# Two gate projections moved over the block boundary, and four Horner steps moved behind the masking products, in a Mamba-2 mixer

## The reference

```
x = x + mixer(layernorm(x))
x = x + mlp(layernorm(x))

mixer:  proj = h @ W_in * mup;  z, xBC, dt = split(proj)          # 1024, 1280 and 64 columns
        xBC = silu(causal depthwise convolution of 4 taps)         # x, B, C
        dt = softplus(dt + dt_bias);  dA = exp(-dt * exp(A_log))
        state = state * dA + (dt * x) outer B;  y = state . C      # 64 heads of 16, state of 128
        g = (y + D * x) * silu(z)
        out = (g * rsqrt(mean(g^2) + eps) * norm_w) @ W_out
mlp:    out = ((silu(h @ gate' * gs) * (h @ up' * us)) @ down') * ds   # inner width 1408
```

## Time and profile before

| | us |
|---|---|
| median of 3 runs | 861.14 (858.68 to 861.72) |
| the profiled execution | 859.09 |
| its span | 857.4 |
| PE busy | 763.8, 89% of the span |
| DVE busy | 525.5, 61% |
| ACT busy | 506.9, 59% |
| POOL busy | 301.3, 35% |

### The profile page before, as it was taken

How to read it: one execution, slowest core, us unless ns; L and a number is a source line. 1 busy time by engine, 2 the same in 40 slices (tenths; PEclk the granted TensorE clock), 3 DMA queues, 4 the chain that set the end, 5 groups by cost and what they waited for, 6 DMA issues and landing times. The chain is left out here.

```text
span 857.4 us, 20336 instructions
## 1 busy us (share of the span) xinstructions
PE 763.8 (89%) x8488; PEld 622.6 (73%) x8488; DVE 525.5 (61%) x840; ACT 506.9 (59%) x963; POOL 301.3 (35%) x247
## 2 busy tenths in 40 slices
PE   5786989989989999998998998554989999999997
PEld 5765778778768777777777776343867887887886
DVE  6865874975965984985985984572832442442341
ACT  6968786887877886887887886412631331331330
POOL 3055284274374364455455454223001101101002
PEclk9968999999999999999999999786989999999999
DMA  9614242452443253243253153752001201201102
GB/s 309 177 40 114 46 115 75 85 124 77 77 107 101 67 117 101 56 125 103 54 125 106 29 124 107 291 213 63 25 2 62 86 1 61 86 0 62 37 1 74
DMA packets 39196, 77.68 MB, mean 91 GB/s; under 512 B 9408, under 2 KB 15040, under 8 KB 39104
## 3 DMA queue, kind: packets, MB, share of 16 engines
q1 hardware_dynamic: 38784, 75.84, 32.0%
q10 hardware_dynamic: 320, 0.52, 0.3%
HBM read 67.43 MB, written 8.92 MB: 89 GB/s over the span
## 5 line engine op out<-in xcount | busy, mean ns | idle before, releaser
L409 POOL TENSOR_TENSOR ring<-tokd,ring 128x1024 f32<-128x1024 f32 x64 | 121.1, 1904 | 229.1 <-ACT tokd L571 190.1
L1051 PE MATMUL ps_proj<-xn_hi,win_hi 128*128 128x256 f32 x608 | 181.6, 299 | 17.5 <-ACT sz L520 13.9
L1052 PE MATMUL ps_proj<-xn_lo,win_hi 128*128 128x256 f32 x608 | 173.9, 286 | 0.0
L1053 PE MATMUL ps_proj<-xn_hi,win_lo 128*128 128x256 f32 x608 | 173.3, 285 | 0.0
L1051 PEld LDWEIGHTS ps_proj<-xn_hi,win_hi 128*128 128x128 f32 x608 | 117.7, 194 | 33.6 <-issue 15.8
L1052 PEld LDWEIGHTS ps_proj<-xn_lo,win_hi 128*128 128x128 f32 x608 | 117.9, 194 | 0.0
L1053 PEld LDWEIGHTS ps_proj<-xn_hi,win_lo 128*128 128x128 f32 x608 | 117.8, 194 | 0.0
L792 DVE SCALAR_TENSOR_TENSOR cx<-cin,consts,cx 128x256 f32<-128x256 f32 x240 | 97.5, 477 | 0.5 <-ACT cx L552 0.4
L1352 POOL TENSOR_TENSOR res<-res,hidden 128x512 f32<-128x512 f32 x16 | 20.5, 1282 | 189.1 <-DVE hidden L1427 189.1
L847 DVE TENSOR_TENSOR ring<-ring,ps_tok 128x1024 f32<-128x1024 f32 x64 | 75.6, 1213 | 17.6 <-ACT ring L580 17.6
L1384 ACT ACTIVATE silu_g<-pb,scales 128x512 f32<-128x512 f32 x44 | 30.3, 688 | 94.4 <-PE pb L1496 94.3
(11 more groups left out here) (150 smaller groups left out, 1530.1 us busy)
## 6 DMA issues: line engine op xcount, KB each, us to landing
ring<-cum_dram SPq DMA_DIRECT2D x128, 256.0 KB, 4.6
xin<-x SPq DMA_DIRECT2D x8, 512.0 KB, 4.1
res<-x SPq DMA_DIRECT2D x32, 128.0 KB, 2.6
x_in_sb<-x_dram SPq DMA_DIRECT2D x4, 1024.0 KB, 6.3
res<-x_dram SPq DMA_DIRECT2D x16, 256.0 KB, 2.6
out<-res SPq DMA_DIRECT2D x16, 256.0 KB, 2.0
x_dram<-res SPq DMA_DIRECT2D x28, 128.0 KB, 2.4
wg<-gate_w SPq DMA_DIRECT2D x4, 704.0 KB, 9.8
```

The costliest lines, as they stand in the source:

```text
L409: pool.tensor_tensor(ring[:, g, :, :], own, ring[:, g, :, :], ALU.subtract).then_inc(diffed, 1)
L1051: pe.matmul(out, win_hi[:, k, cols], xn_hi[:, k, :], start=(k == 0), stop=False)
L1052: pe.matmul(out, win_hi[:, k, cols], xn_lo[:, k, :], start=False, stop=False)
L1053: made = pe.matmul(out, win_lo[:, k, cols], xn_hi[:, k, :], start=False, stop=(k == KT - 1))
```

## The change

Three things move, and nothing is added or removed.

PE: `project(i, 6)` and `project(i, 7)` stood behind `turn_tok(i, 0)` and behind `turn_x(i, 0)` in their own block. They now stand at the end of the block before, behind its last `project_out`. `project(i, 8)` stood behind `group(c, 0)` and now stands before `carry(i, 0)`.

ACT: `evacuate(i, 6)` and `evacuate(i, 7)` stood behind the last `fade` of step 2i. `evacuate(i, 6)` is now the first instruction of the block, `evacuate(i, 7)` follows `square`, and `keep_tok` stands behind that. The first two clamps are ahead of `square`.

DVE: the Horner steps 4 to 7 stood between `mask_cb` and `make_xpad` of the second step. They now stand behind the four `mix` products, together with steps 8 to 11.

```
@@ scalar body @@
                 c = STEPS * i
-                keep_tok(c)
+                if not first:
+                    evacuate(i, 6)
                 clamp(c, 0)
+                clamp(c, 1)
                 if not first:
                     square(c - 1)
-                clamp(c, 1)
+                    evacuate(i, 7)
+                keep_tok(c)
                 fade(c, 0)
...
                 fade(c, 3)
-                if not first:
-                    evacuate(i, 6)
-                    evacuate(i, 7)
-                else:
+                if first:
                     for n in range(EARLY, PIECES):
@@ vector body @@
                 mask_cb(c)
-                for n in range(4, 8):
-                    soft(i + 1, n)
                 make_xpad(i, 1)
...
                 for g in range(1, GROUPS):
                     mix(c, g)
-                for n in range(8, LOGN):
+                for n in range(4, LOGN):
                     soft(i + 1, n)
@@ tensor body @@
                 turn_tok(i, 0)
-                if not first:
-                    project(i, 6)
                 turn_x(i, 0)
-                if not first:
-                    project(i, 7)
+                if first:
+                    pe.wait_ge(lo_made, EVENTS)
+                project(i, 8)
                 carry(i, 0)
...
                 group(c, 0)
-                if first:
-                    pe.wait_ge(lo_made, EVENTS)
-                project(i, 8)
                 group(c, 1)
...
                 project_out(c - 1, SECOND_HALF)
+                if not last:
+                    project(i + 1, 6)
+                    project(i + 1, 7)
```

## The result

The changed kernel takes 828.59 us (median of four runs, 826.47 to 829.62), the kernel before 861.43 (four runs, 858.68 to 861.8): a ratio of 0.962, 95% interval 0.959 to 0.965. The forecast was 836, and its range ended at 829. The gain is 32.8 us where I had 25.4; between the two profiled executions it is 859.09 - 829.62 = 29.5 us. Direction and mechanism came as forecast, the size did not. Of all executions behind the ratios of this document, two (1186 us of a later kernel, 1445 us of the kernel before) were in a slow state and are not counted in them.

A forecast was written before the change was run, and what follows sets the result against it. TensorE was taken as the bound, with two recurring holes. 13.9 + 8.9 + 3.0 - 2.8 - 1 + 3.4 = 25.4 us off 859.1 gave 833.7; with 2.05 added for the median, 836 us (831 to 840).

The forecast's parts named there:

- The wait for `sz`: TensorE before project(i,8), waiting for ScalarE's evacuation of a gate pair: all seven waits go, 13.9 us.
- that for `xpad` in blocks 1 to 6: TensorE before carry(i,1): the 1.46 us wait goes once Horner steps 4 to 7 move, 8.9 us in six blocks.
- block 0's: Block 0's `xpad` wait before its second carry: 4.20 us falls to some 1.2, a gain of 3.0 us.
- ACT's new order: ScalarE: keep_tok 5.19 us after gate_hi; rival: keep_tok 1 to 2 us later, 843 to 850 us, chance 0.09.
- At 68.07 in block 0: Block 0: keep_tok behind clamps and project(0,8) before a slow carry delay pair 8; 1 us lost, bounds 0 and 2.5.
- three signs of "wrong": Wrong if carry(i,0) waits over 1 us, eight Horner steps take over 3.5 us, or new stalls exceed 5 us.
- the step headed "Sum": Whole kernel: 13.9 + 8.9 + 3.0 - 2.8 - 1 + 3.4 = 25.4 us saved.
- "Nothing is added": TensorE: no work added; 48 matmuls (6.0 us) move to the block before and project(i,8) moves ahead of the carry.
- The new wait: TensorE before carry(i,0), for `xpad` behind the later keep_tok: 0.4 us seven times, 2.8 us lost.
- The clock: Slow TensorE stretches behind waits in blocks 1 and 4 and at a carry: 3.4 us gained, bounds 0 and 4.3.
- More stalls: Rival, TensorE's steady part: two more "issue" stalls, 3.1 us each plus 1.4 us slow clock, 845 us; chance 0.12.
- The steps beside POOL: Rival, VectorE: fade_state slows the eight Horner steps to 0.76 us each, 861 us (chance 0.04), or 892 (0.02).

The follow-up runs named there:

- the gate part alone: The changed kernel with Horner steps 4 to 7 put back ahead of `xpad`, so without the DVE move: 841.47 us, ratio 0.979 against the kernel before.

## Why the prediction was right in kind and 7.4 us short

**Right, with its numbers.** The wait for `sz` went (13.9 us), that for `xpad` in blocks 1 to 6 too (8.9), and block 0's fell from 4.20 to 1.30 us (2.9, forecast 3.0). ACT's new order had the slots that I gave it (5.15 us to keep_tok, forecast 5.19), no table load came between, and the steps missed fade_state by 0.6 us. At 68.07 in block 0 0.85 us were lost, for which 1 was taken. Each of the three signs of "wrong" stayed away: no wait over 1 us at carry(i,0), eight steps in 2.57 us, and no more stalls than before.

**Where it failed: the step headed "Sum".** The starts of turn_tok(1,0) and turn_tok(7,0), before and after:

```profile
109.59 0.27 PE L1081 MATMUL ps_tok<-eye,cx 128*128 128x128 f32 x1
...
502.82 0.27 PE L1081 MATMUL ps_tok<-eye,cx 128*128 128x128 f32 x1
```

```profile
112.04 0.27 PE L1079 MATMUL ps_tok<-eye,cx 128*128 128x128 f32 x1
...
481.58 0.27 PE L1079 MATMUL ps_tok<-eye,cx 128*128 128x128 f32 x1
```

turn_tok(1,0) starts 2.45 us later (109.59, then 112.04), but two projections, some 5.8 us, have moved ahead of it, so 3.3 us were gained there (forecast 3.1). From there to turn_tok(7,0) it gained 393.23 - 369.54 = 23.7 (forecast 20.4), and behind that 8.3 less the same 5.8 = 2.5 (forecast 1.9). So 4.1 us are missing from the sum, 3.3 of them in the steady part:

- *"Nothing is added" on TensorE was taken as "the work keeps its length".* It does not. Block 4 is 5.30 us shorter, and its waits and its slow projection give 2.26 + 1.46 + 1.45 - 0.24 = 4.93; the other 0.37 us are starts that lie closer. Projections 6 and 7 take 2.84 us each in the changed kernel, from one start to the next (353.69, 356.53, 359.36), where in the kernel before they took 2.95 behind turn_tok and 3.00 behind turn_x. What stands ahead makes the difference: behind an output product (as 6 now does) or another projection (as 7 does) the second matmul starts 0.12 us after the first, behind turn_tok, turn_x or a group 0.20 to 0.23. Groups 0 and 1 in a row take 308.84 to 310.25 = 1.41 us, apart 0.79 + 0.80. In six blocks 2.2 us are left over, of which 0.7 are the stall, shorter by chance or by a cause that no run shows (2.42 us for 3.13); the closer starts are the other 1.5 us: the largest term that was missing.
- *The new wait* was 0.72, 0.23, 0, 0.24, 0.24, 0.47 and 0.24 us, in all 2.1 for a forecast of 2.8; 0.5 of it in the six blocks.
- *The clock.* I took 3.4 of the 4.3 us, "as block 0 keeps a wait". It keeps 1.30 us, and the carry behind it ran in 1.94 us, at full clock: the upper bound was right, and 0.5 us more of it fell to the steady blocks than I had in the sum.

The new neighbours of projections 6 and 7 were in the order of instructions, and the spread of projection lengths, 2.95 to 3.09 us by what stands ahead and behind, was in the trace; I did not ask where it came from.

**The other 3.1 us are not in the mechanism.** I added 2.05 us, since the profiled execution of before lay that far under the median. The changed kernel's profiled execution lay 1.03 above its own median. The second profiles took 859.99 and 829.29 us, and the kernel before ran between 854.3 and 863.7 us in its undisturbed runs. That is scatter of single executions, and nothing allowed it to be carried over as a constant with its sign: without it the forecast is 833.7, against 829.62 of the profiled execution. Taken from the medians alone, my 25.4 would have given 861.43 - 25.4 = 836, and with the 4.1 us 832; the last 3.3 us to 828.59 are in no trace, and by the spread of the runs they can be scatter.

**What the sum hid.** I added the terms as if each could be had alone. The runs show that they can't: the Horner part alone is worth 0 us, the gate part alone 18, and all but project(i,8)'s move 0. That the sum came as near as it did has luck in it. The forecast came near only because all of it was done at once and every chain that could have taken the place of a hole (keep_tok, the last gate, the end of the second half) moved with it.

**The rivals.** More stalls: not seen; the stall sits at the same instruction in all but one of the kernels whose waits are shown here, the `turn_tokd` in the second half of block 2 with 5 of 16 products to go (turn_tokd(3,0) in the program; the expectations above call it turn_tokd(4,0)). ACT's new order: not seen. The steps beside POOL: the mechanism is real, 23 us when it is brought about, and 0.6 us of distance kept it away here. Its price per step was wrong (one long wait, not eight slow steps), and it left out what the clock adds.

What stays open: why a wait of about 2.2 us was followed by a slow clock in two or three cases of six in one kernel, a wait of 2.1 us in seven of seven in another, and one of 2.72 us in a third not at all; and what the stall is. One thing in the traces bears on it: in all ten profiles that have the stall, a 16 KB packet of the DMA queue that the profile calls "instruction" starts 2.6 to 2.8 us before the products go on, and takes 1.3 us; in the one without it, the packet starts 4.9 us before the transposition. That the products wait for it is a guess that no run tests.

## What to carry to other kernels

Where several waits recur in one loop, find which chain would be late next before adding them up: the first fix may be worth nothing alone and the second most of it. When a step moves, its new neighbours on the same engine count too, since an instruction can start sooner behind one than behind another. Look at what the products behind each TensorE wait take, and price the wait with them, and leave the distance between one profiled execution and the median out of the sum unless it repeats.

## What was not expected of the hardware

- A vector instruction that meets a POOL instruction can be held for all that is left of it: 3.76 us, in two blocks, and 2.88 us in five for a Horner step of 0.29 us beside fade_state. GPSIMD Engine Reference of the Trainium skill, Specifications, has the contention that this agrees with; that it takes one instruction whole, and leaves the others as they are, is what the run shows.
- The cost of a hole is not its length, nor is it settled by it. In the steady blocks the granted clock was low behind two or three of six waits of 2.2 us, behind all six of 2.65 us, all six of 3.1 us and more, and, ahead of a carry, all seven of 2.1 us; behind waits of up to 1.5 us, the one of 1.90 and the one of 2.72 us ahead of a carry it was not. In the kernel with the Horner part alone the windows (us; busy us and count of PE, PEld, DVE, ACT, POOL; granted clock; DMA share; GB/s) show one projection at half clock and one at full:

```profile
321.75:327.23 5.48, 5.48 (x32) 5.26 (x38) 1.69 (x5) 2.99 (x10) 1.23 (x3) 0.50 0.15 34
306.04:309.14 3.10, 3.10 (x29) 3.10 (x27) 2.03 (x2) 1.00 (x2) 3.10 (x2) 1.00 0.02 5
```
